# Row sums taken beside the attention products, the router taken into the norm loop, and the residual tile loaded in bfloat16

## The reference

```python
Q = (x @ Wq.T).reshape(B, S, H, DH).transpose(0, 2, 1, 3)   # 32 heads of 128
K = x @ Wk.T                                                # one shared head
V = x @ Wv.T
# sliding window of 512 at a stride of 256, sigmoid in place of softmax
attn = jax.nn.sigmoid(scores)
attn = attn / jnp.sum(attn, axis=-1, keepdims=True)
wout = jnp.einsum('bhqk,bkd->bhqd', attn, Vw)
blended = (1.0 - alpha) * out[:, :, i:oe] + alpha * wout[:, :, :oe - i]
# second half: a dense layer plus a mixture of low-rank experts, top 2 of 8
base = jnp.einsum('bsd,od->bso', x, base_W)
mid = jnp.einsum('bsd,edr->bser', x, lora_A) * w_dense[..., None]
y = base + jnp.einsum('bser,erd->bsd', mid, lora_B) * SCALING
# around them
x = x + _layernorm(attention(_layernorm(x)))
x = x + _layernorm(ffn(_layernorm(x)))
```

## Time and profile before

| | us |
|---|---|
| median of three runs | 2661.81 (2661.43 to 2662.63) |
| the profiled execution's own time | 2659.0 |
| its span, slowest core (5) | 2657.2 |
| spans of the 8 cores | 2633.6 to 2657.2 |
| mean granted TensorE clock, by core | 0.867 to 0.881 |

### The profile page before, as it was taken

How to read it: one execution, slowest core, us unless ns; L and a number is a source line. 1 busy time by engine, 2 the same in 40 slices (tenths; PEclk the granted TensorE clock), 3 DMA queues, 4 the chain that set the end, 5 groups by cost and what they waited for, 6 DMA issues and landing times.

```text
span 2657.2 us, 49124 instructions; the slowest of 8 cores (2633.6 to 2657.2 us)
## 1 busy us (share of the span) xinstructions
PE 1960.7 (74%) x20000; PEld 1681.3 (63%) x20000; DVE 592.3 (22%) x1560; ACT 656.9 (25%) x1143; POOL 89.2 (3%) x59
## 2 busy tenths in 40 slices
PE   1357999999988888873999999611146999999400
PEld 0237999999856666662888888500035888888400
DVE  2431222222233333330000000345531000000344
ACT  3650111111155454540111111243410111111111
POOL 1000000000000000001000000000000000000000
PEclk9999999999977788886999999855557999999755
DMA  9721555665200000008457456132250654564233
GB/s 211 194 96 33 64 65 69 79 77 65 33 2 2 2 2 2 2 2 80 64 67 93 65 77 84 48 126 99 107 80 1 85 75 64 78 83 64 79 154 146
DMA packets 226423, 187.31 MB, mean 70 GB/s; under 512 B 18720, under 2 KB 220448, under 8 KB 220448
## 3 DMA queue, kind: packets, MB, share of 16 engines
q0 software_dynamic: 214256, 104.96, 32.1%
q1 hardware_dynamic: 11952, 79.22, 8.0%
HBM read 263.97 MB, written 25.17 MB: 109 GB/s over the span
## 4 chain that ended last, share of the span: by engine, by line
PE 66%; DVE 10%; ACT 8%; DMA 8%; issue 7%; DVEq 1%; ACTq 0%; SPq 0%; POOL 0%; POOLq 0%
PE ps_all L758 17%; PE ps_all L644 17%; PE ps_all L439 17%; PE ps_all L554 4%; DVE bn L263 3%; DMA xstage<-x_ext 2%; ACT sig L504 2%; PE ps_all L529 2%; PE ps_all L490 2%; DMA xre<-x_ext 2%; DMA out<-outstage 2%; PE ps_all L295 1%; ACT xt_stage L282 1%; DVE bl L567 1%; DMA slab<-woT 1%
## 5 line engine op out<-in xcount | busy, mean ns | idle before, releaser
L644 PE MATMUL ps_all<-slab,attn_T 128*128 128x256 bf16 x4096 | 449.1, 273 | 41.7 <-DMA slab<-woT 41.7
L439 PE MATMUL ps_all<-slab,ln1T_own 128*128 128x256 bf16 x4096 | 469.6, 273 | 0.6 <-ACT krT L374 0.6
L758 PE MATMUL ps_all<-slab,ln2T 128*128 128x256 bf16 x4096 | 463.7, 273 | 0.8 <-ACT midgT L744 0.8
L644 PEld LDWEIGHTS ps_all<-slab,attn_T 128*128 128x128 bf16 x4096 | 401.6, 98 | 89.1 <-issue 41.8
L758 PEld LDWEIGHTS ps_all<-slab,ln2T 128*128 128x128 bf16 x4096 | 401.9, 98 | 48.7 <-issue 1.0
L439 PEld LDWEIGHTS ps_all<-slab,ln1T_own 128*128 128x128 bf16 x4096 | 396.2, 98 | 45.1 <-issue 0.8
L504 ACT ACTIVATE sig<-ps_all,kbias_s 128x512 bf16<-128x512 f32 x384 | 225.9, 726 | 202.4 <-PE ps_all L490 202.4
L554 PE MATMUL ps_all<-v_sb,sig 128*128 128x128 bf16 x2048 | 181.8, 266 | 22.4 <-DVE bl L575 21.9
L554 PEld LDWEIGHTS ps_all<-v_sb,sig 128*128 128x128 bf16 x2048 | 165.8, 123 | 33.6 <-issue 32.5
L295 PE MATMUL ps_all<-identB,xt2stage 128*128 128x128 bf16 x256 | 34.0, 301 | 202.0 <-ACT xt2stage L282 190.1
L490 PE MATMUL ps_all<-qrT,krT 128*128 128x256 bf16 x768 | 137.2, 281 | 53.0 <-ACT sig L504 52.2
(11 more groups left out here) (85 smaller groups left out, 1450.3 us busy)
## 6 DMA issues: line engine op xcount, KB each, us to landing
slab<-wqT POOLq DMA_DIRECT2D x16, 2048.0 KB, 22.1
slab<-woT POOLq DMA_DIRECT2D x16, 2048.0 KB, 15.9
slab<-baseT POOLq DMA_DIRECT2D x16, 2048.0 KB, 15.7
xstage<-x_ext SPq DMA_DIRECT2D x12, 2048.0 KB, 13.9
xre<-x_ext SPq DMA_DIRECT2D x8, 2048.0 KB, 7.5
out<-outstage SPq DMA_DIRECT2D x8, 2048.0 KB, 6.3
x_scratch<-x1b SPq DMA_DIRECT2D x8, 1024.0 KB, 3.9
x1re<-x_scratch SPq DMA_DIRECT2D x8, 1024.0 KB, 5.2
```

The lines of the kernel that those rows point to most:

```text
L439: return e.matmul(reg, ln1T_own[:, d, t * 128:(t + 1) * 128], slabs[par][:, d, :], start=(d == 0), stop=(d == 31))
L644: return e.matmul(reg, attn_T[:, d, t * 128:(t + 1) * 128], slabs[par][:, d, :], start=(d == 0), stop=(d == 31))
L758: return e.matmul(reg, ln2T[:, d, t * 128:(t + 1) * 128], slabs[par][:, d, :], start=(d == 0), stop=False)
```

## The change

Three things are done.

**Attention.** Each step is cut into two halves of two heads. In a half, every 128-column matmul (new L542) is followed by the one-column matmul with the same weights (new L551). The reciprocal and the product with alpha are done once per half, on 8 columns (new L560, L565), and the eight blends of the half come behind them. The row sums take a PSUM bank of the ring twice per step. The table of alphas is stored in the matching order.

**Norm loop and router.** The router's work on tile t is emitted right behind the transposes of tile t, inside the norm loop. `xre` becomes bfloat16 (the DMA casts), no longer shares its memory with `xt2stage`, and is loaded by POOL's queue as soon as the sum of the tile before has been taken.

**Dense layer.** The experts' second factor comes as a piece of 256 columns with each slab (`brider`). The dense tiles use two PSUM banks instead of four and wait for their own tile's `midgT`.

The diff, cut to its core:

```diff
-    xre    = sb("xre", (128, D), F32, FREG)
+    xre    = sb("xre", (128, D), BF16, FREG)
-    xt2stage= sb("xt2stage", (128, D), BF16, FREG + 0)
+    xt2stage= sb("xt2stage", (128, D), BF16, FREG + 8192)
...
+        if rider:
+            def f2(e, s=s, par=par):
+                return e.dma_start(out=brider[par][:, :], in_=b_all[:, s * OC:(s + 1) * OC])
+            P.op("gpsimd", f2, inc=s_slab[par], inc_by=16)
...
+        for half in range(2):
+            rbank, rbw = sc_ring.acquire()
...
+            for h4 in (2 * half, 2 * half + 1):
+                bk = 2 + (h4 & 1)
+                for win in (0, 1):
+                    for qh in range(2):
...
+                        for jj in range(4):
...
+                            P.op("tensor", fa, waits=w0,
+                                 inc=(s_av if (win == 1 and jj == 3) else None))
...
+                            P.op("tensor", fr, inc=(s_av if lastr else None))
...
+            P.op("vector", lambda e, rbank=rbank, uoff=uoff: e.reciprocal(
+                    ur16[:, uoff:uoff + 8], rbank[:, 0:8]),
+                 waits=[(s_av, r_end), (s_u, s_u.n)], inc=s_chain)
...
+            for h4 in (2 * half, 2 * half + 1):
...
+                av_free[h4 & 1] = [(s_bl, s_bl.n)]
...
     for t in range(NT):
-        P.op("sync", fx, waits=[(s_pev, pev_counts[t]), (s_xre, s_xre.n),
-                                (s_chain, s_chain.n), (s_tpe, s_tpe.n)],
+        P.op("gpsimd", fx, waits=[(s_pev, pev_counts[t]), (s_chain, last_add[0])],
              inc=s_xre, inc_by=16)
...
         ln2t_counts.append(s_tpe.n)
+        emit_router(t)
...
-    y_ring = Ring([ps[0], ps[1], ps[2], ps[3]], init_conds=[(s_mgT, MG_DONE)])
+    y_ring = Ring([ps[2], ps[3]], init_conds=[(s_pev, D_MM)])
-        par, c_slab = emit_slab_load(baseT, s)
+        par, c_slab = emit_slab_load(baseT, s, rider=True)
```

More of the change, by code:

```diff
@@ L191, in build_program @@
     midgT    = sb("midgT", (128, NT, 128), BF16, FREG + 41472)
-    midg  = [sb(f"midg_{i}", (128, 128), BF16, FREG + 43520 + 256 * i) for i in range(2)]
+    midg  = [sb(f"midg_{i}", (128, 128), BF16, FREG + 45568 + 256 * i) for i in range(2)]
+    brider = [sb(f"brider_{i}", (128, OC), BF16, FREG + 43520 + 512 * i) for i in range(2)]
     wex      = sb("wex", (128, 128), F32, FREG + 44544)
@@ L513, in emit_rav_main @@
         sbuf_sig = sig[sp]
[L514 to L543, removed]
-        binfo = []
[L545 to L548, removed]
-                for qh in range(2):
[L550 to L584, removed]
@@ L696, in build_program, with emit_router @@
     first_w16 = [True]
-    for t in range(NT):
+    mgT_counts = {}
+    m_free_l = [m_free]
+    def emit_router(t):
         for d in range(32):
@@ L702, in build_program @@
             P.op("tensor", f,
-                 waits=(list(m_free) + [(s_fw2, FW2_N), (s_tpe, ln2t_counts[t])]) if d == 0 else ())
+                 waits=(list(m_free_l[0]) + [(s_fw2, FW2_N), (s_tpe, ln2t_counts[t])]) if d == 0 else ())
             def f2(e, d=d, t=t):
@@ L736, in build_program @@
         c_mg = s_chain.n
-        m_free = [(s_chain, c_mg)]
+        m_free_l[0] = [(s_chain, c_mg)]
         tb, tw = mg_ring.acquire()
@@ L760, in build_program, with finc @@
                 P.op("tensor", f,
-                     waits=(yw + [(s_slab[par], c_slab), (s_mgT, MG_DONE), (s_fw, FW_N)]) if d == 0 else ())
-            def finc(e, t=t, s=s, reg=reg):
-                return e.matmul(reg, midgT[:, t, :], b_all_s[:, s * OC:(s + 1) * OC],
+                     waits=(yw + [(s_slab[par], c_slab), (s_mgT, mgT_counts[t])]) if d == 0 else ())
+            def finc(e, t=t, reg=reg, par=par):
+                return e.matmul(reg, midgT[:, t, :], brider[par][:, :],
                                 start=False, stop=True)
@@ L840, in _host_inputs @@
                 a = np.ones(256, dtype=np.float32)
-            for qh in range(2):
-                for h4 in range(4):
-                    alpha_a[:, c * 16 + (0 * 2 + qh) * 4 + h4] = 1.0 - a[qh * 128:(qh + 1) * 128]
-                    alpha_a[:, c * 16 + (1 * 2 + qh) * 4 + h4] = a[qh * 128:(qh + 1) * 128]
+            for half in range(2):
+                for qh in range(2):
+                    for h4b in range(2):
+                        alpha_a[:, c * 16 + half * 8 + (0 * 2 + qh) * 2 + h4b] = 1.0 - a[qh * 128:(qh + 1) * 128]
+                        alpha_a[:, c * 16 + half * 8 + (1 * 2 + qh) * 2 + h4b] = a[qh * 128:(qh + 1) * 128]
         in_maps.append({
```

98 lines of the change are left out of this document (94 added, 4 removed).

## The result

The changed kernel takes 2739.07 us (median of 10 runs) against 2661.42 us for the kernel before in the same comparison. The ratio is 1.029, with a 95% interval of 1.0279 to 1.0301: 77 us slower. Some runs of either kernel, one of ten before and two of ten after, took 5 to 10% longer on part of the cores; the ratios leave them out. The profiled execution took 2736.7 us, its slowest core (0) 2734.8 us; the cores lie between 2716.2 and 2734.8 us, with mean clocks of 0.860 to 0.867. The kernel before had its slowest profile on core 5, this one on core 0, so the positions of rows in the span don't match one for one.

The account below looks back on a forecast made before the run. PE is full in the slab stages; the change touches attention and the norm loop, where engines wait for one another. Attention 55 us plus norm loop 11 us, 66 us on 2661.8, gives 2728 us; range 2700 to 2755 us.

Parts of the forecast that it names:

- The wait between the halves: Attention: PE waits before head 2 for head 0's blends, which need the half's reciprocal; 2.75 us per step.
- the mix of before: Attention: 39% of the front at the lower clock level, kept unchanged; mean front 9.4 us, 1.6 us more per step.
- the front: Attention step from first row sum to first score: 7.83 us mean before, 9.4 us forecast.
- the back: Attention step from first score to next row sum: 6.95 us, set by ACT's sigmoid passes, left alone by the change.
- The last two steps: End of attention: no scores cover the blends; 2.2 us each laid bare, 4 us in all.
- Pairs: Attention: product plus thin matmul cost 0.08 us at the upper clock, 0.13 at the lower; pairing itself gains and costs nothing.
- rival E: Attention: thin matmul rides for nothing, pairs cost 0.055 us, clock stays up; front 7.1 us, total 2654 us; chance 5%.
- The norm loop: Norm loop and router: period 43.9 us against 29.8, 19.5 us slower, less 8.4 us from the bfloat16 sum: 11 us.
- Rival B: Norm loop: bf16 sum runs at double rate, all else as forecast; stage costs 2.5 us, total 2719 us; chance 26%.
- my middle value of 3.4 us: Norm loop: bfloat16 residual sum taken between 2.3 and 4.43 us, giving 8.4 us back over 8 tiles.
- Rivals C: Attention: the clock recovers, fronts of 8.3 us, total 2692 us; chance 13%.
- D: Attention: the bare wait drops the clock in every step, fronts of 11.2 us, total 2785 us; chance 10%.

Follow-up runs that it names:

- Experiment 3: Changed kernel with 46 further 128-column matmuls on TensorE between the two halves of each attention step: 2713.81 us, ratio 1.0205 to the kernel before.
- Experiment 2: Kernel before with only the change's norm loop, router and dense layer, attention as before: 2658.43 us, ratio 0.9996.
- Experiment 7: Kernel before with only the norm part of the change, but the router's work put back behind the norm loop: 2622.1 us, ratio 0.9863.
- Experiments 4: Changed kernel with a PSUM bank for each of the four heads: 2634.67 us, ratio 0.991 to the kernel before.
- 5: Kernel before with a PSUM bank for each head, row sums still in one block ahead of the products: 2639.43 us, ratio 0.9925.
- 6: Changed kernel, two halves and two banks, each half's 32 row sums in one block ahead of its products: 2627.39 us, ratio 0.9878 to the kernel before.
- 10: Kernel before with attention in halves, row sums in a block, a bank per head, and the norm part with router behind the loop: 2594.24 us, ratio 0.9742.

## Why the prediction was right, and where its sizes were off

**The wait between the halves** came where it was put, 32 times, with the releaser named. I summed it to 2.75 us; it is 2.90 us. Most of the difference is the step from the product with alpha to the first blend, 0.41 us where I put 0.28.

**The clock.** This is the term that was mis-sized. I kept the mix of before for the whole front and gave it 9.4 us. The mean clock over a front did stay about the same (0.77 and 0.71 on cores 0 and 5 before, 0.75 and 0.76 after; the 0.82 that I set beside my mix was that of the whole stage), but it is not spread: the first half runs at 0.96 in the mean, the second at 0.53, and the level falls in or right behind the wait. So the front adds up as 2.7 us of first half, 2.9 of wait and 4.2 of second half to the first score, 9.8 us. What I had left at 6.95 us, the back, grew to 7.23 us: after the slow half the first scores start at the lower level too. Experiment 3 shows cause and effect: with matmuls in the gap the second half runs at 1.00 and takes 2.9 us, and the back 7.0. The rule of the Trainium skill, "TensorE: Matmul & The Clock Gate", Part 1, that activity releases a throttle which is otherwise on, agrees: 46 matmuls more per step, and the kernel was 25 us faster.

**The last two steps.** I gave them 2 x 1.6 us like every step and 4 us for the bare blends, 7.2 us. They cost (14.50 - 10.79) + (15.71 - 10.44) = 9.0 us. Together: 30 x (2.08 + 0.29) = 71 us for the steps and 9 us for the end make the 80 us, where I had 55. Of the 25 us between, 14 are the front, 9 the back and 2 the end.

**Pairs.** They cost 0.08 us (2.60 us for the 32 of a first half) and 0.13 us as the router's rows said, so rival E fell: the thin matmul does not ride for nothing.

**The norm loop.** The order on DVE made the period 41.1 us, as I had it less the faster sum: 43.9 us with the old sum and 41.8 with one of 2.29 us. Rival B holds for the sum: 2292 ns, near the low end that I had taken by the widest operand. The Trainium skill, "VectorE: DVE Perf Modes", "The perf-mode tier table", has such a sum at twice the float32 rate, and the trace agrees; my middle value of 3.4 us was wrong. First transpose to dense layer came out at 305.2 us against 305.4, where I had 11 us more; the sum explains 8.5 of them, and the period was shorter than my terms by another 0.7 us. Experiment 2 confirms it: no difference to be measured. Experiment 7 shows what was behind the even account, a gain of some 37 us from the early load and the sum together, and the same loss from the router's place.

**Rivals C and D.** The clock neither recovered nor fell throughout. Each half took its own side.

**In sum**, 2728 us was forecast and 2739 measured: 25 us too little for attention, 11 too much for the norm part. The two errors cancelled in part, so the nearness of the total is partly luck: in the norm part rival B's term came true, and B's own total, 2719 us, lies further off.

**What stays open.** Experiments 4, 5, 6 and 10 take the wait away in different ways, and all end at 13.60 to 13.70 us per step, each with a part of the front at a lower clock. Why they meet there is not settled. Nor is it known why the loads were slower in experiment 3.

## What to carry to other kernels

When work is interleaved so that two results finish together, look at what hangs on the one that used to finish early: here the row sums were thin, but their reciprocal stood ahead of every blend, and the blends ahead of a bank. A bare wait on TensorE can be paid twice, once as a wait and once in what follows at the lower clock; here some 1.3 and 0.8 us per front. To price the clock, compare stretches at the same level: the kernel before has a clock of its own. And a part that comes out even can hide a gain and a loss of the same size: split it before it is dropped.

## What the runs showed of the hardware that I had not expected

- The clock of one stretch by its neighbour: a gap of 2.9 us on TensorE was followed by a half at 0.50 in the step shown, and 0.53 over all steps and cores. With the gap filled the same half was at 1.00 in all 240 steps and cores.
- A two-source sum over 4096 columns took 2292 ns with all operands bfloat16 in SBUF and 4426 ns with one of them float32, while the statistics took 678 ns per 512 columns for either type.
- Issuing the casting load of `xre` took POOL 0.53 us (median), a slab's 1.68 us; it landed in 10.0 us, the float32 load by SP's queue in 7.5 us.
